# Part of a gather moved from GpSimd to SyncE, with the start, the seam and the selection rounds reordered

## The reference, cut to what matters

```
def _gcn(x, W, b, src, dst, w, n):
    h = x @ W
    agg = jax.ops.segment_sum(w[:, None] * h[src], dst, num_segments=n)
    return agg + b

f1 = layernorm(x)
h  = _gcn(f1, W1, b1, src, dst, values, N)
y  = leaky(concat([h, f1[root]]))
y  = leaky(_gcn(y, W2, b2, src, dst, values, N))
x1 = x + leaky(concat([y, h[root]]) @ Wl + bl)

z = layernorm(x1)
weights = z @ wr + br
sel = the rows of z with the k-1 largest weights
x2 = x1 + z + (gelu(sel @ w1 + b1) @ w2 + b2) * weights   # last term for selected rows only
```

## Time and profile before

| | us |
|---|---|
| median of 3 runs | 2100.82 |
| the profiled execution's own time | 2107.75 |
| its span, first to last instruction | 2106.0 |
| first layer's gathers from `normed_rows`, start of the first to start of the last | 76.2 to 1022.1 |
| second layer's gathers from `conv_rows`, start of the first to start of the last | 1041.8 to 2026.5 |
| POOL busy | 1514.8 (72%) |
| PE busy | 1686.5 (80%) |
| DVE busy | 1136.2 (54%) |
| ACT busy | 373.3 (18%) |

### The profile page before, as it was taken

One profiled execution on the slowest core, in us unless ns is written; L12 is line 12 of the kernel. 1 busy time (PEld: TensorE's weight loads), 2 busy tenths in 40 slices (PEclk: granted clock), 3 DMA queues, 4 the chain that ended last, 5 costly groups with the idle time before them and its releaser, 6 DMA issues.

```text
span 2106.0 us, 39360 instructions
## 1 busy us (share of the span) xinstructions
PE 1686.5 (80%) x7147; PEld 1351.4 (64%) x7148; DVE 1136.2 (54%) x4017; ACT 373.3 (18%) x921; POOL 1514.8 (72%) x1609
## 2 busy tenths in 40 slices
PE   1588876777767776766689999999998989898886
PEld 0466655655545555554468888877887777677665
DVE  8666454444434333333266666665665656555556
ACT  6211000001000000000012222222222222222221
POOL 7677777777777777777477777777777777777730
PEclk9999898898988888788699999999999999999998
DMA  8933333333333333333233333333333333333313
GB/s 270 316 112 110 112 110 111 110 110 111 109 112 112 110 112 109 112 112 110 78 105 105 103 105 105 104 103 104 103 105 104 104 105 104 104 104 104 104 57 122
DMA packets 113372, 242.23 MB, mean 115 GB/s; under 512 B 29013, under 2 KB 62740, under 8 KB 113338
## 3 DMA queue, kind: packets, MB, share of 16 engines
q0 software_dynamic: 75200, 205.10, 33.9%
q1 hardware_dynamic: 28444, 29.03, 4.3%
q10 hardware_dynamic: 9694, 7.77, 1.2%
HBM read 222.42 MB, written 19.38 MB: 115 GB/s over the span
## 4 chain that ended last, share of the span: by engine, by line
POOL 44%; PE 25%; issue 18%; DVE 7%; DMA 3%; DVEq 2%; ACT 0%; ACTq 0%; POOLq 0%
POOL ring L360 44%; PE ps_agg L613 15%; PE ps_up L737 3%; PE ps_dn L726 3%; DMA ring<-normed_rows,idx 2%; DMA ring<-conv_rows,idx 1%; DVE S L1012 1%; PE ps_o L694 1%; DVE xs L1280 1%; DVE fw2s L934 1%; DVE acc L1020 1%; PE ps_dn L724 1%; PE ps_o L691 1%; PE ps_o L772 1%; DVE fw2s L952 0%
## 5 line engine op out<-in xcount | busy, mean ns | idle before, releaser
L613 PE MATMUL ps_agg<-ring,S 128*128 x3136 | 863.5, 424 | 363.7 <-DVE S L1012 136.0
L613 PEld LDWEIGHTS ps_agg<-ring,S 128*128 128x128 f32 x3136 | 639.3, 210 | 526.7 <-issue 433.7
L360 POOL DMA_INDIRECT ring<-conv_rows,idx x782 | 747.6, 956 | 256.7 <-issue 232.8
L360 POOL DMA_INDIRECT ring<-normed_rows,idx x752 | 718.0, 955 | 239.6 <-issue 221.0
L1020 DVE TENSOR_TENSOR acc<-acc,ps_agg x490 | 206.4, 421 | 621.5 <-PE ps_agg L613 571.5
L1012 DVE TENSOR_SCALAR S<-iota,dstc,wc 128x128 f32<-128x128 int16 x1584 | 448.7, 363 | 157.3 <-issue 125.8
L613 PE MATMUL ps_agg<-ring,S_more 128*128 x768 | 197.6, 403 | 20.1 <-DVE S_more L1012 13.8
L726 PE MATMUL ps_dn<-fw2s,hT 128*128 128x256 f32 x848 | 209.1, 401 | 0.0
L613 PEld LDWEIGHTS ps_agg<-ring,S_more 128*128 128x128 f32 x768 | 153.4, 204 | 58.7 <-issue 35.5
L726 PEld LDWEIGHTS ps_dn<-fw2s,hT 128*128 128x128 f32 x848 | 163.5, 199 | 40.3 <-issue 18.9
L737 PE MATMUL ps_up<-xnT,fw1s 128*128 128x256 f32 x800 | 183.1, 382 | 1.5 <-ACT hT L471 1.5
(11 more groups left out here) (211 smaller groups left out, 1028.3 us busy)
## 6 DMA issues: line engine op xcount, KB each, us to landing
ring<-conv_rows,idx POOLq DMA_INDIRECT x782
ring<-normed_rows,idx POOLq DMA_INDIRECT x752
conv_rows<-rows ACTq DMA_DIRECT2D x50, 128.0 KB
xs<-in_x SPq DMA_DIRECT2D x4, 1280.0 KB, 18.2
normed_rows<-xs SPq DMA_DIRECT2D x3, 1280.0 KB, 6.9
xs<-in_x SPq DMA_DIRECT2D x4, 896.0 KB, 15.7
out_rows<-xs SPq DMA_DIRECT2D x3, 1024.0 KB
xs<-in_x SPq DMA_DIRECT2D x2, 1152.0 KB
```

The costliest lines, as they stand in the source:

```text
L360: pool.indirect_dma_start(out=ring[:, slot * TG + t, :], out_offset=None, in_=rows_of, in_offset=bass.IndirectOffsetOnAxis(ap=idx[:, tile: ...
L613: last = nc.tensor.matmul(to, select[:, t, :], moving, start=(t == 0), stop=(t == TG - 1))
```

## The change

1. **Gather.** In every third round (16 rounds of each layer), the last tile of quarter 1 is no longer gathered by POOL. SP loads it row by row: it reads the 128 byte offsets from a table `far` into registers, 32 at a time, and issues one DMA of 1 KB per row, into one of two extra slots of `ring`. A tile's readiness is signalled to PE behind the first 32 rows of the next one. Issue of tile n waits until tile n - 2 is used. The table costs one more DMA on ACT and two small operations on DVE; the table of windows also holds the slot of each round's last tile, which is four more small operations on DVE and some register arithmetic in PE's and DVE's loops.
2. **Start.** x is loaded and stored in nine chunks, not six. POOL scales quarters 0 and 2 of the first batch and ACT quarters 1 and 3. DVE enters the rounds behind the first batch: statistics of groups 4 and 5 are taken ahead of round 0, those of groups 6 and 7 and the chain of the second batch behind round 0. The late weights are loaded by ACT, behind its scaling of the second batch.
3. **Seam.** DVE, PE and ACT do the steps of the window before the last one ahead of the last window's sums, and the last W2 product goes to another bank.
4. **Selection rounds.** Each round takes one piece of feed-forward work.

```diff
-        ring = sb("ring", [P, SLOTS * TG, D])
+        ring = sb("ring", [P, SLOTS * TG + FAR_SLOTS, D])
+        far = sb("far", [FARS, P], i32)
...
-        XCH = [(39, NW), (29, 39), (19, 29), (14, 19), (7, 14), (0, 7)]
+        XCH = [(39, NW), (29, 39), (24, 29), (19, 24), (14, 19), (10, 14), (7, 10), (3, 7), (0, 3)]
...
+            def far_tile(l, rows_of, n, b, before):
+                k = within(sp.snap(n * -1 + (FARS - 1)), FARS - 1)
+                sp.wait_ge(group_used[l], n * (FAR_EVERY * QG) + 1)
+                for c in range(P // FAR_PASS):
+                    _, offsets = nc.values_load_multi_w_load_instructions(
+                        bass.at_runtime_partition(far[0:1, c * FAR_PASS:(c + 1) * FAR_PASS], k), engines=(mybir.EngineType.SP,),
...
+                    for i in range(FAR_PASS):
+                        p = c * FAR_PASS + i
+                        sp.dma_start(ring[p:p + 1, SLOTS * TG + b, :].bitcast(i8), rows_of[ds(offsets[i], D * 4)].unsqueeze(0)).then_inc(far_landed[l][b], 16)
+                    if c == 0 and before is not None:
+                        far_done(l, 1 - b, before)
...
-                        pool.wait_ge(group_used[l], g - SLOTS + 2)
-                    for t in range(TG):
+                        pool.wait_ge(group_used[l], g - SLOTS + 2 + USED0)
+                    by_sp = q == FAR_Q and it > 0 and it % FAR_EVERY == 0
+                    for t in range(TG - 1 if by_sp else TG):
...
-            rounds((stage_step0, turned_step0, rows_step0, y_step0), NW)
-            rows_step0(NW)
+            rounds((stage_step0, turned_step0, rows_step0, y_step0), NW - 1)
+            rows_step0(NW - 1)
+            stage_step0(NW - 1)
+            turned_step0(NW - 1)
+            y_step0(NW - 1)
+            rows_step0(NW, ps_dn)
...
-                for _ in range(1 if r < 2 else 2):
-                    next(pieces, None)
+                next(pieces)
...
-            row_stats(0)
-            row_stats(1)
+            row_factors(0, [row_sums(0, q) for q in range(QG)][-1])
...
+                if l == 0:
+                    for q in range(2):
+                        row_sums(1, q)
...
+                dve.sem_inc(group_used[l], USED0)
...
+                if l == 0:
+                    with dve.Fori(0, 1) as it:
+                        edge_round(l, it, None)
+                    row_factors(1, [row_sums(1, q) for q in range(2, QG)][-1])
```

More of the change, by code:

```diff
@@ L347, in _ @@
                         pool.wait_ge(raw_stats, 1)
[L348 to L351, removed]
+                        for part in range(0, QG, 2):
+                            for t in RAW_TILES[0][part * TG:(part + 1) * TG]:
+                                last = nc.gpsimd.tensor_scalar(ring[:, t, :], ring[:, t, :], raw_rstd[:, t:t + 1], raw_nmr[:, t:t + 1], ALU.mult, ALU.add)
+                            last.then_inc(raw_first[part], 1)
                         for stored in f_stored:
@@ L411, in _, with scale_rows @@
             normalise_rows(1)
+            def scale_rows(tiles):
+                for t in tiles:
+                    last = nc.scalar.activation(ring[:, t, :], ring[:, t, :], ACT.Identity, scale=raw_rstd[:, t:t + 1], bias=raw_nmr[:, t:t + 1])
+                return last
+            act.wait_ge(raw_stats, 1)
+            for part in range(1, QG, 2):
+                scale_rows(RAW_TILES[0][part * TG:(part + 1) * TG]).then_inc(raw_first[part], 1)
             act.wait_ge(raw_stats, 2)
[L413 to L414 removed]
+            last = scale_rows(RAW_TILES[1])
             last.then_inc(raw_second, 1)
+            act.wait_ge(diag_ready, 1)
+            act.wait_ge(edges_turned, 3)
+            for scaled in raw_first:
+                act.wait_ge(scaled, 1)
+            act.wait_ge(raw_second, 2)
+            for to, of in big_loads[2:]:
+                act.dma_start(to, of).then_inc(late_weights, 16)
             act.wait_ge(consts_ready, 4)
@@ L708, in _ @@
                 pe.sem_inc(s, 1)
-            rounds(0, (no_step, turn_step0, h_step0, no_step), NW, first_root_term)
-            second_layer(NW)
+            rounds(0, (no_step, turn_step0, h_step0, no_step), NW - 1, first_root_term)
+            second_layer(NW - 1)
+            turn_sums(0, NW - 1)
+            h_step0(NW - 1)
+            nc.tensor.matmul(ps_dn[:, 0:D], ones[0:1, :], rootrow[0:1, :], start=True, stop=False)
+            pe.wait_ge(z_ready[0], NW + 1)
+            for k in range(KC):
+                last = nc.tensor.matmul(ps_dn[:, 0:D], zT[:, k, :], W2s[:, k, :], start=False, stop=(k == KC - 1))
+            last.then_inc(o_done[0], 1)
+            pe.wait_ge(o_kept[0], NW + 2)
             pe.wait_ge(late_weights, 16 * (N_WEIGHTS - 2))
```

111 lines of the change are left out of this document (78 added, 33 removed).

## The result

The changed kernel takes 2078.15 us, median of 4 runs (2076.78 to 2078.42); the kernel before takes 2100.42 beside it, median of 4 (2099.37 to 2104.38). The ratio is 0.9891 [0.9879, 0.9902]: 22 us faster, 1.1%, well clear of the 0.3% that a measurement can tell. Predicted were 2066 and 2048 to 2110: the sign is right, the gain is two thirds of the forecast's 34.2 us, and the time lies just above the forecast's own range (2054 to 2076). The profiled execution has an own time of 2076.78, a span of 2075.0 and a mean clock of 0.931.

The account below looks back on a forecast made before the run. POOL's gathers were taken to bound both layers. First layer -10.6, second -20.1, seam -2.5, end -1 sum to -34.2 us: 2073.5 own time, median 2066. Range 2048 to 2110; the forecast's own range 2054 to 2076.

Parts of the forecast that it names:

- What bounds the kernel: Both layers: POOL's gathers, 1.254 us each, set the pace; 16 fewer save 20.1 us per layer if SP delivers in time.
- PE binds the second layer: Rival: PE is full in the second layer, which then gains nothing, for 2087 us; chance 0.07.
- T: SP's time per tile of 128 row DMAs and four loads: 54 us, ends 41 and 113.
- one price per value: SP's loads: a load costs 0.302 us for each value, making a tile 87 us and the time 2970; 8 in 100.
- Break-even: SP's time per tile at which the change gains nothing: 58.3 us first layer, 61 second, 59.8 over all.
- That case: Rival: SP is slower than POOL and sets the layers; each us per tile beyond 59.8 costs 32 us; chance 0.21.
- The start: First layer's opening: DVE enters rounds without the second batch, POOL reaches group 12 at 95.3 instead of 96.4, gaining 1.1 us.
- a stall of POOL at the first tile: First layer, near 148 us: SP's first tile is ready at 147.5, so POOL waits 10.6 us for group 21's slot.
- The reordered head: Start of first layer: second batch's statistics behind round 0; gain 1.1 us, ends -6.8 and +4.
- Seam: Between the layers: the last W1 product goes ahead of the last sums, 2.5 us less (0 to 4).
- End: After the last gathers: rounds of one feed-forward piece end sooner but six pieces go behind; gain 1 us, ends -4 and +3.
- Own time and median: Step from the execution's own 2073.5 us to the predicted median: runs' median taken as 6.9 us lower, 2066.6.

Follow-up runs that it names:

- e12: Changed kernel with every load of 32 addresses done twice in SP's tiles: 2153.59 us, ratio 1.0251 to the kernel before.
- e3: Changed kernel without SP's gather, so POOL gathers all tiles; new head, seam and selection rounds stay: ratio 1.0012 to the kernel before.
- e1: Changed kernel, but PE itself gives the credit that lets it pass quarter 1 ahead of SP's first tile: ratio 0.9883 to the kernel before.
- e11: As e2, but the 11 reloads of x follow SP's last first-layer tile and tiles 0 and 1 are signalled once landed: 2065.53 us, ratio 0.9827.
- e0: Kernel before with one more register operation per group on PE and DVE and one on the loaded lag: 2107.52 us, ratio 1.0004.
- e2: As e1, but SP issues and signals its first tile of the first layer ahead of the 11 reloads of x: ratio 0.9849 to the kernel before.

## Why the prediction was right, and where it missed

- **What bounds the kernel.** Right. POOL's gathers set both layers, and 16 fewer took 20.9 us from the second layer between first and last gather (20.1 predicted; 20.4 to 22.3 over the pairs of first and second executions). "PE binds the second layer" is out: no such loss.
- **T.** Right within 6%: 50.9 to 52.0 us against 54, by two errors that partly cancel. A row has 0.225 + 0.029 and its gaps, (131.2 - 80.3 - 4 x 2.07)/128 = 0.333 us, for 0.38. A load of 32 takes 2.07 us, not 1.14; the loads are 8.3 us, not 4.6. The branch of one price per value is out, and the Trainium skill's 200 ns per register (Runtime: NRT & Kernel Launch, Instruction fetch mechanics) isn't borne out here for loads from SBUF: 2071/32 = 65 ns.
- **Break-even.** Not contradicted: 59.8 predicted, 59.5 from e12 with the predicted slope. That case decides between -1% and +2.5% over 9 us of T, and a slower chip alone is enough to get into it.
- **The start: the step that failed.** I put 9.5 us there (-1.1 for the head and +10.6 for a stall of POOL at the first tile); it cost 13.6. All of it is there when POOL starts group 12, and it has other parts than mine: 96.42 before, 98.79 with the new head alone (e3), 110.03 with SP's credit, so +2.4 for the head and +11.2 for the credit, and nothing for the tile. The stall near 148 that I named as a sign didn't come. I did not see that PE's group 1 also waits for a word from SP that needs no tile, and that SP says it behind 17 us of reloads. That the credit's 11.2 lies so near to my 10.6 is luck. The stall itself is real, but stands behind the credit: e1, without the credit, has it, at 13.5 us. There the tile came 1.0 us later than I had it and POOL reached group 12 3.3 us later, which shortens the stall; but from the tile to the slot it took 7.4 us and not 2.3, since the group's tiles are multiplied a second time for its other window and PE came back from its wait at half speed (3.78 us for a sum of 1.99). What the two waits share is SP's place in its own queue, and e11 shows that moving the reloads out of it gives 14 us of the layer back.
- **The reordered head.** Predicted 1.1 gained. With reloads in flight it loses: POOL's group 12 comes 2.4 us later in e3 than in the kernel before. The hold comes a group earlier than I had it (group 11), since DVE gives group 3's slot back in its step of group 4, behind the second chain and the root row. I had followed ACT's scaling to group 4 and left out what DVE does itself, its unexplained gap of 6.5 us above all.
- **Seam.** Predicted 2.5, and the two first profiled executions show 3.0. That they agree is luck: the difference is TensorE's clock in that stretch. The product does move ahead; the time to the last stored row doesn't measurably shrink.
- **End.** Predicted 1; from the last gather to the end are 79.5 and 78.8 us before, 79.0 and 81.5 changed: nothing to be seen.
- **Small slips.** In the second layer, group 21 comes behind 83 gathers, not 81 (104 us), and the stalls given there for T = 50 and 57 are those of the first layer's first tile. Neither changes the sum.
- **Own time and median.** The own times differ by 31.0 us, 34.2 were predicted. The medians differ by 22.3. I had carried over that the profiled execution of the kernel before was 6.9 us above its median; that of the changed kernel was 1.4 below. This took 8.3 of the 12 us between 2066 and 2078, more than all terms together, and 3 us of it are the seam's clock. Profiling adds nothing fixed: the second one of the kernel before (e0) was 1.7 below its median.

What the gain is made of, in ratios: without SP's gather +0.1%, with it -1.0 to -1.1%, with SP's reloads out of its way -1.7%.

## What to carry to other kernels

When work moves to an idle engine, look up everything that the engine has queued ahead of its first delivery, and put there only what someone waits for: moving eleven DMAs that nobody needed for 900 us, together with the credit and the signals of two tiles, was worth 15 us, two thirds of the change's gain again. A helper engine paced near its break-even is a bet on the machine: with 12% of its period in hand it won 1.1%, some 9 us more per tile lost 2.5%, and on a slower chip it lost 11.6%, so measure its slack per period, and on more than one chip. Take away one of two waits of which either is enough, and nothing moves; and compare medians with medians, since one profiled execution can lie 7 us off.

## What the runs showed of the hardware

- SP issues a DMA of one 1 KB row from an address in a register every 0.33 us (0.225 for the DMA, 0.029 for a move), steadily over 4096 of them: from a tile's first load to its last row are 50.1 to 50.7 us for each of the 32 tiles, while POOL gathers at 1.254 us beside it.
- A load of 32 registers from one SBUF row takes 2.07 us on SP; a load of one took 1.14 on SP and 0.302 on PE.
- DVE stood without a shown releaser ahead of its first instruction behind the second chain: 6.5 us with the DMA engines' share at 1.04 to 1.09 from 66 to 84 us (e1, e3), 3.5 with 0.17 to 0.41 (e2, e11).
- Measurements differ by chip: the kernel before took 2100 to 2102 us in three, 2107 in a fourth, each a median of 4 to 23 runs, and 2644 (11 runs) in the last, where the changed kernel's trace shows the same durations on SP, POOL and DVE as elsewhere and longer gaps between instructions.
